# Recommendation tower on one core: a second GpSimd chunk in each third layer, the top MLP on pairs of tiles

## What is computed

```python
x0 = xk = e                       # (2048, 32, 16), gathered rows
outs = []
for W in (W0, W1, W2):            # (32, 32, 64), (32, 64, 64), (32, 64, 64)
    xk = relu(einsum('bmd,bhd,mhk->bkd', x0, xk, W))
    outs.append(sum(xk, axis=2))  # over the 16 dims
h = concatenate([outs..., dense_ctx], axis=1)      # 192 + 16
h = maximum(h @ W_top1 + b_top1, 0.0)              # 512
h = maximum(h @ W_top2 + b_top2, 0.0)              # 256
y = h @ W_top3                                     # 1
```

## Time and profile before

| what | us |
|---|---|
| median of 3 runs (lowest, highest) | 1177.24 (1174.41, 1178.77) |
| the profiled execution, whole | 1176.1 |
| the profiled execution, span of its instructions | 1174.3 |

### The profile page before, as it was taken

One profiled execution on the slowest core, in us unless ns is written; L12 is line 12 of the kernel. 1 busy time (PEld: TensorE's weight loads), 2 busy tenths in 40 slices (PEclk: granted clock), 3 DMA queues, 4 the chain that ended last, 5 costly groups with the idle time before them and its releaser, 6 DMA issues.

```text
span 1174.3 us, 15688 instructions
## 1 busy us (share of the span) xinstructions
PE 1123.1 (96%) x5370; PEld 399.2 (34%) x5370; DVE 1114.6 (95%) x511; ACT 822.5 (70%) x2259; POOL 913.6 (78%) x639
## 2 busy tenths in 40 slices
PE   0779999999999999999999999999999999999998
PEld 0222223333333333333333333333333333333343
DVE  1679999999999999999999999999999999999995
ACT  0346656867868686786877868587776859678674
POOL 6788788888888888888888888888888888885400
PEclk9999999999999999999999999999999999999999
DMA  6788657876666786667787766678766668866300
GB/s 146 206 205 171 133 116 165 174 156 135 132 143 145 166 175 143 137 126 149 149 174 154 150 138 138 135 163 174 153 143 133 141 143 166 174 144 138 66 1 1
DMA packets 78335, 167.31 MB, mean 142 GB/s; under 512 B 22096, under 2 KB 39904, under 8 KB 78256
## 3 DMA queue, kind: packets, MB, share of 16 engines
q1 hardware_dynamic: 59248, 157.76, 61.3%
q0 software_dynamic: 16384, 4.23, 3.8%
q10 hardware_dynamic: 2624, 4.34, 1.3%
HBM read 157.86 MB, written 8.40 MB: 142 GB/s over the span
## 4 chain that ended last, share of the span: by engine, by line
PE 87%; POOL 5%; DVE 3%; issue 3%; ACT 2%; DMA 0%; SPq 0%; DVEq 0%; POOLq 0%
PE acc L762 81%; POOL x_rows L347 4%; DVE p_dve L657 3%; PE acc L866 3%; ACT xb L415 2%; PE acc L852 1%; PE acc L854 1%; PE acc L874 1%; DVE z L684 0%; POOL p_pool L374 0%; ACT x_s L423 0%; ACT xa L406 0%; DMA first_s<-in_first_row 0%; ACT out_l L519 0%; ACT h L550 0%
## 5 line engine op out<-in xcount | busy, mean ns | idle before, releaser
L762 PE MATMUL acc<-p_dve,w_s 128*64 128x512 f32 x3840 | 855.6, 595 | 19.8 <-DVE p_dve L657 19.7
L347 POOL DMA_INDIRECT x_rows<-in_table,ids_s x512 | 492.7, 962 | 146.2 <-issue 131.8
L657 DVE TENSOR_TENSOR p_dve<-spread,xb 128x3072 f32<-128x3072 f32 (+2 forms) x225 | 566.0, 2572 | 3.9 <-issue 3.9
L657 DVE TENSOR_TENSOR p_dve<-spread,xa 128x2048 f32<-128x2048 f32 (+1 forms) x192 | 495.5, 2634 | 9.5 <-ACT xa L406 4.3
L762 PEld LDWEIGHTS acc<-p_dve,w_s 128*64 128x64 f32 x3840 | 271.2, 137 | 554.7 <-issue 485.7
L415 ACT ACTIVATE xb<-acc 32x512 f32<-32x512 f32 x512 | 288.8, 564 | 49.0 <-DVE p_dve L657 42.6
L363 POOL TENSOR_TENSOR p_l<-spread,q_tile 128x2048 f32<-128x2048 f32 x59 | 268.5, 4580 | 8.4 <-DMA q_tile<-x_of_steps 7.4
L406 ACT ACTIVATE xa<-acc 64x512 f32<-64x512 f32 x256 | 145.9, 570 | 158.2 <-PE acc L762 116.9
L374 POOL TENSOR_TENSOR p_pool<-spread,x_s 128x1024 f32<-128x1024 f32 x64 | 152.3, 2379 | 89.3 <-PE acc L762 47.1
L423 ACT ACTIVATE x_s<-acc 64x512 f32<-64x512 f32 x256 | 151.3, 591 | 11.7 <-ACT y_row L569 4.7
L762 PE MATMUL acc<-p_l,w_s 32*64 32x512 f32 (+1 forms) x600 | 139.7, 601 | 0.0
(11 more groups left out here) (26 smaller groups left out, 233.3 us busy)
## 6 DMA issues: line engine op xcount, KB each, us to landing
spread<-x_of_steps SPq DMA_DIRECT2D x244, 512.0 KB, 16.9
q_tile<-x_of_steps SPq DMA_DIRECT2D x120, 128.0 KB
x_rows<-in_table,ids_s POOLq DMA_INDIRECT x512, 4.4
x_of_steps<-x_rows SPq DMA_DIRECT2D x60, 128.0 KB, 1.8
spread<-x_of_steps ACTq DMA_DIRECT2D x4, 512.0 KB, 10.7
spread<-x_of_steps SPq DMA_DIRECT2D x6, 256.0 KB, 5.2
w_s<-in_w SPq DMA_DIRECT2D x2, 512.0 KB, 5.8
spread<-x_of_steps SPq DMA_DIRECT2D x8, 128.0 KB, 3.2
```

Source lines behind the costliest of these rows:

```text
L347: nc.gpsimd.indirect_dma_start(out=x_rows[:, s % 2, i * DIM:(i + 1) * DIM], out_offset=None, in_=table, in_offset=bass.IndirectOffsetOnAxi ...
L657: nc.vector.tensor_tensor(p_dve[:, to:to + n, :], spread[:, s % 3, tile:tile + n, :], over(x[:], n), ALU.mult).then_inc(dve_made, n)
L762: last = nc.tensor.matmul(halves(acc[b * K:(b + 1) * K, :]), w, of_block(prod, b), start=start, stop=stop)
```

## The change

Five edits in one:

1. POOL makes chunks 6 and 7 of layer 3, not 7 alone, from step 1 on; `p_pool` becomes a ring of two. DVE makes 14 chunks there. PE takes both POOL chunks behind chunk 11.
2. `p_dve` has nine slots, not ten. As 15 + 14 products a turn don't fit it, DVE's instruction is cut in two where it would cross the ring's end.
3. ACT takes the first layer's sums of all steps from 4 on; their second half is moved behind `out_1`.
4. The squares are computed on all 128 partitions, with zero weights for the 96 that aren't needed.
5. The MLP works on pairs of tiles (256 columns): tile 0 alone, seven pairs, tile 15 alone. A pair's work is four parts, one to a turn, behind chunk 5 of layer 2: two halves of the first MLP layer (8 matmuls each), the second (16), the third (2). The matmuls of a pair have 64 columns of weights and 256 of data.

```diff
-POOL_CHUNK = NT - 1
-CD = CL - 1
-RING = 10
+RING, POOL_RING = 9, 2
...
-GROUPS_L2 = [(0, 2), (2, 3), (5, 2), (8, 3), (11, 1), (12, 2), (14, 2)]
+GROUPS_L2 = [(0, 2), (2, 3), (5, 1), (8, 3), (11, 1), (12, 2), (14, 2)]
+GROUPS_L2_OF_0 = [(0, 2), (2, 3), (5, 2), (8, 3), (11, 1), (12, 2), (14, 2)]
...
-MLP1_AFTER, MLP2_AFTER, MLP3_AFTER = 5, 5, 13
+LAST_GROUP = TILES // 2
+MLP_AFTER = 5
...
-LATE_MLP1_AFTER, LATE_MLP2_AFTER, LATE_MLP3_AFTER = 4, 15, 6
+LAST_PAIR_AFTER = {1: 0, 9: 1}, {4: 2, 12: 3}
+def mlp_part_of_turn(s):
+    group, part = divmod(s - 4, 4)
+    return (group, part) if s >= 4 and (group, part) != (0, 3) else None
...
 def sums_by_act(s):
-    return s % 2 == 1 and s >= 5
+    return s >= 4
...
+def pool_chunks(s, layer):
+    return (NT - 2, NT - 1) if layer == 2 and s > 0 else (NT - 1,)
...
-        p_pool = sb("p_pool", [P, COLS])
+        p_pool = sb("p_pool", [P, POOL_RING, COLS])
...
             def product(s, layer):
-                n = pool_from(s, layer)
                 pool.wait_ge(x1s_ready if layer == 1 else x2s_ready, s + 1)
                 if layer == 1:
                     pool.wait_ge(b_loaded[s % 3], 16 * Q * (s // 3 + 1))
-                if n > 0:
-                    pool.wait_ge(pool_used, n)
-                nc.gpsimd.tensor_tensor(p_pool[:], spread[:, s % 3, POOL_CHUNK, :], x_s[:, layer - 1, :],
-                                        ALU.mult).then_inc(pool_made, 1)
+                for n, c in enumerate(pool_chunks(s, layer), pool_from(s, layer)):
+                    if n >= POOL_RING:
+                        pool.wait_ge(pool_used, n + 1 - POOL_RING)
+                    nc.gpsimd.tensor_tensor(p_pool[:, n % POOL_RING, :], spread[:, s % 3, c, :],
+                                            x_s[:, layer - 1, :], ALU.mult).then_inc(pool_made, 1)
...
-                nc.scalar.activation(p_l0[0:FIELDS, CP, :], q_tile[0:FIELDS, :],
-                                     ACT.Square).then_inc(squares_made, 2)
+                nc.scalar.activation(p_l0[:, CP, :], q_tile[:], ACT.Square).then_inc(squares_made, 2)
...
-                if sums_by_act(s):
-                    sums_0(s, 1)
...
                 if s >= 1:
                     x2_s(s - 1)
                     out_1(s - 1)
+                if sums_by_act(s) and s + 1 < STEPS:
+                    sums_0(s, 1)
...
             def products(s, layer, c, n):
-                i = dve_from(s, layer) + dve_slot(c)
-                if i + n > RING:
-                    dve.wait_ge(dve_used, i + n - RING)
+                i = dve_from(s, layer) + dve_slot(s, layer, c)
                 to, tile = i % RING, c % NT
+                if to + n > RING:
+                    products(s, layer, c, RING - to)
+                    products(s, layer, c + RING - to, n - (RING - to))
+                    return
+                if i + n > RING:
+                    dve.wait_ge(dve_used, i + n - RING)
...
                 if c == (POOL_AFTER_L2 if s > 0 else POOL_AFTER_L2_OF_0):
-                    pe.wait_ge(pool_made, pool_from(s, 2) + 1)
-                    contract(acc2, w2_s[:, POOL_CHUNK, :], p_pool[:], False, False
-                             ).then_inc(pool_used, 1)
+                    for n, chunk in enumerate(pool_chunks(s, 2), pool_from(s, 2)):
+                        pe.wait_ge(pool_made, n + 1)
+                        contract(acc2, w2_s[:, chunk, :], p_pool[:, n % POOL_RING, :], False, False
+                                 ).then_inc(pool_used, 1)
...
+            def blocks(out, terms):
+                for i, (w, x) in enumerate(terms):
+                    for b in range(2):
+                        last = nc.tensor.matmul(out[b * K:(b + 1) * K, :], w[:, b * K:(b + 1) * K], x,
+                                                start=i == 0, stop=i == len(terms) - 1)
+                return last
...
+            def mlp_pair(step, group, part):
+                if part < 2:
+                    z_is_there(group)
+                acc0_is_free(step, mlp_before(group) + part)
+                for n in range(2):
+                    out = acc0[:, n * 2 * P:(n + 1) * 2 * P]
+                    if part < 2:
+                        cols = slice((2 * part + n) * P, (2 * part + n + 1) * P)
+                        last = blocks(out, ((wt1[:, 0, cols], z_all[:, 0, :]),
+                                            (wt1[0:TOP, 1, cols], z_all[0:TOP, 1, :])))
+                    elif part == 2:
+                        last = blocks(out, [(wt2[:, k, n * P:(n + 1) * P], h1[:, k, :])
+                                            for k in range(H1 // P)])
+                if part == 3:
+                    last = last_layer(2 * P)
                 last.then_inc(mlp_made, 1)
```

More of the change, by code:

```diff
@@ new lines, in evict, with store_y @@
+            def evict(group, part, h, chunks, bias, n_cols):
+                act.wait_ge(mlp_made, mlp_before(group) + part + 1)
+                for i, n in enumerate(chunks):
+                    last = nc.scalar.activation(h[:, n, 0:n_cols], acc0[:, i * n_cols:(i + 1) * n_cols], ACT.Relu,
+                                                bias=bias[:, n:n + 1])
+                last.then_inc(mlp_done, 1)
+            def store_y(group, part, n_cols):
+                n = mlp_before(group) + part + 1
+                act.wait_ge(mlp_made, n)
+                nc.scalar.activation(y_row[:, 0:n_cols], acc0[0:1, 0:n_cols], ACT.Copy).then_inc(mlp_done, 1)
+                act.wait_ge(mlp_done, n)
+                tiles = tiles_of(group)
+                act.dma_start(y[:, tiles.start * P:tiles.stop * P], y_row[:, 0:n_cols]).then_inc(y_stored, 16)
@@ L602, in _ @@
                     squares(s + 1)
-                if t >= 0 and even:
-                    mlp1(t)
-                if t >= 0 and not even:
-                    mlp2(t)
-                if sums_by_act(s):
-                    sums_0(s, 1)
+                if mlp_part_of_turn(s):
+                    group, part = mlp_part_of_turn(s)
+                    (mlp_pair if group > 0 else mlp_single)(group, part)
                 if s == STEPS - 1:
@@ L613, in _ @@
                     x2_b(s - 1)
+                if s == STEPS - 1:
+                    mlp_pair(LAST_GROUP - 1, 0)
                 if s == 1:
                     squares(2)
-                if t >= 0 and not even:
-                    mlp3(t)
                 if s >= 1:
@@ L638, in _ @@
             move_z2(TILES - 1)
-            mlp1(TILES - 1)
-            mlp2(TILES - 1)
-            mlp3(TILES - 1)
-            act.wait_ge(y_stored, 16 * TILES)
+            for part in range(3):
+                mlp_single(LAST_GROUP, part)
+            act.wait_ge(y_stored, 16 * (LAST_GROUP + 1))
         @block.vector
@@ L773, in layer0 @@
                 for c in CP, *range(CP):
-                    rows = P if c < CP else FIELDS
                     if c == CP:
@@ new lines, in mlp_single @@
+            def mlp_single(step, group, part):
+                t = tiles_of(group).start
+                if part == 0:
+                    z_is_there(group)
+                acc0_is_free(step, mlp_before(group) + part)
+                if part == 0:
+                    for n in range(H1 // P):
+                        cols = slice(n * P, (n + 1) * P)
+                        nc.tensor.matmul(acc0[:, cols], wt1[:, 0, cols], z_all[:, 0, z_cols(t)],
+                                         start=True, stop=False)
+                        last = nc.tensor.matmul(acc0[:, cols], wt1[0:TOP, 1, cols], z_all[0:TOP, 1, z_cols(t)],
+                                                start=False, stop=True)
+                elif part == 1:
+                    for n in range(H2 // P):
+                        cols = slice(n * P, (n + 1) * P)
+                        for k in range(H1 // P):
+                            last = nc.tensor.matmul(acc0[:, cols], wt2[:, k, cols], h1[:, k, 0:P],
+                                                    start=(k == 0), stop=(k == H1 // P - 1))
+                else:
+                    last = last_layer(P)
@@ L884, in _ @@
             for s in range(STEPS):
-                t = s // 2 - 2
-                even = s % 2 == 0
                 for c in range(CL):
                     layer1(s, c)
-                    if t >= 0 and even and c == MLP1_AFTER:
-                        mlp1(t)
-                    if t >= 0 and not even and c == MLP2_AFTER:
-                        mlp2(t)
-                    if t >= 0 and not even and c == MLP3_AFTER:
-                        mlp3(t)
+                    if c == MLP_AFTER and mlp_part_of_turn(s):
+                        group, part = mlp_part_of_turn(s)
+                        (mlp_pair if group > 0 else mlp_single)(s, group, part)
                     if s == 0 and c in L0_OF_1_AFTER:
```

247 lines of the change are left out of this document (129 added, 118 removed).

## The result

The changed kernel takes 1211.15 us (median of 4 runs, 1210.39 to 1214.69) against 1176.7 us for the kernel before in the same comparison: a ratio of 1.0297, 95% interval 1.0273 to 1.0322. By that ratio it is 3.0% slower. The profiled execution has a span of 1209.9 us; the prediction's sum for that span was 1207.6.

The account below looks back on a forecast made before the run. PE set the pace, DVE level, POOL one microsecond a turn to spare. With POOL's turn at 35.88 us, 1134.9 + 71.7 + 1.0 gave a span of 1207.6, with 1.8 around it 1209.4; predicted 1210 us, range 1200 to 1220.

Parts of the forecast that it names:

- the prediction's sum: Whole kernel: third chunk of the last first layer at 1134.9, plus 71.7 to the end, plus 1.0, a span of 1207.6.
- step on POOL: Steady part: one product more lengthens POOL's turn from 33.53 to 35.88 us, above PE's 33.75, so POOL sets the pace.
- 11 us of "idle" in two turns: POOL, steady part: busy shares show 11 us to spare, but waits leave one a turn; pauses between gathers fill the rest.
- loop over DRAM: POOL's inputs: no loop is longer than POOL's own turn; `q_tile` lands 33.2 us into a turn, needed at 35.9.
- 1.8 and 3.7 forecast: PE: times in us claimed for the 256-column MLP parts, the big one being 32 records at 0.115.
- 33.7 a turn, as forecast: PE, steady part: it needs 33.75 us a turn (33.6 to 34.1), 0.8 less than the period before.
- the forecast 2.1 us: PE, first layer and behind chunk 11 of layer 3: waits for POOL of about 2.1 us a turn together.
- the third rival: PE's clock falls after idling: one fall a turn stays hidden, two make PE's turn 37.1 and 1245 us; chance 3%.
- the second: POOL and DVE shut each other out: each new POOL product stops DVE for 2.35 us, at worst 1232 us; chance 2%.
- +1.0 less the squares' 0.3: Tail: MLP records cost 8.4 us against 7.5, +1.0; wider squares take away up to 0.3 of PE's time.

Follow-up runs that it names:

- one_pool_chunk: The changed kernel with edit 1 undone, so POOL makes one chunk of layer 3 again: 1173.74 us, ratio 0.9972 to the kernel before.
- pool_alone_c: The kernel before with edits 1 and 2 alone (second POOL chunk, rings of nine and two): 1209.50 us, ratio 1.0268.
- ring9_alone: The kernel before with only the rings changed, nine slots for DVE and two for POOL: 1213.69 us, ratio 1.0029 on a late-starting chip.
- gather15: The changed kernel with 15 gathers a step in place of 16 from step 2 on: 1178.03 us, ratio 1.0009 to the kernel before.

## Why the prediction was right

Its step on POOL decided it and held to 0.04 us: a turn of 35.92 for 35.88, turn 3 at 155.7 for 155.5, turn 29 at 1089.5 for 1088.4. one_pool_chunk and pool_alone_c show the cause from both sides: without the second chunk 37 us are gone; with it and the rings alone the kernel takes 1209.50, within 2 us of the changed one, and the rings alone cost at most a fraction of that (ring9_alone, 1.0029).

The sum was 2.3 us short of the span. Turn 29 came 1.1 late, and 1.0 of that was left when PE reached the third chunk of the last first layer, at 1135.9 (1133.27 + 3 x 0.86) for 1134.9; the other 1.3 are in the tail. That 1210 lies within 1.2 us of 1211.15 is in part luck: 0.6 was added to the sum's 1209.4 because the profiled execution of before lay below its median, and that of the changed kernel, 1211.75, lies 0.6 above its own.

The reading behind it, that 11 us of "idle" in two turns hide only 2, held: gather15 shows the pauses to be part of a gather's cost. The chain of waits of the changed kernel gives 29% of the span to DMA (`q_tile` above all) and might have spoken for a loop over DRAM; one_pool_chunk changes no DMA and is 37 us faster, so that loop doesn't set the pace.

PE: parts of 16 and 32 records took 1.74 and 3.45 us for the 1.8 and 3.7 forecast, the last part 0.96 for 0.56 (`L955`, 1153.11 to 1154.07), which makes 33.7 a turn, as forecast. PE's idle is less than the forecast 2.1 us: it is busy for 68.32 of 71.80 us (600.00 to 671.80), so idle for 1.7 a turn. The starts give more: from 628.88 to 642.45 PE takes 13.57 us for 52 records, 11.16 us of work at 0.2146 each, so 2.4 are lost in this turn; the profile shows 1.75 of them as idle. Its clock stayed at 1.00 in the steady part (mean of the run 0.997), so the third rival didn't come about. Nor did the second: POOL's products last 2354 to 2402 ns in all 95 cases, and DVE's of 3072 columns 3355 at most, as before.

The Trainium skill (SBUF - State Buffer, "Who interferes with whom") has two-input DVE instructions contend with GpSimd ones that read SBUF. The changed kernel has 31 more such products beside DVE's, none stretched; the trace disagrees with the page, as before.

The tail cost 2.1 us more than before (76.6 from the last first layer to the end, against 74.5), for +1.0 less the squares' 0.3: the last MLP part, twice 0.96 for 0.56, and a wait of 0.70 for ACT (`out_l`, at 1180.77) are most of the rest.

A later theory of mine fell in part. That a turn takes the longer of PE's and DVE's needs is right with nine slots (34.7 expected, 34.74 found) and wrong with ten (34.45 expected, 34.32 found; 34.15 at least, and 34.10). One slot is 0.86 us of PE's work, and the needs alternate by 0.7 to 1.7 us.

## What to carry to other kernels

An engine's slack is the waits that end in front of its instructions, summed over a turn, not one minus its busy share: here 1.0 us against an apparent 5.5. Before work is moved to an engine, add it to that engine's turn and compare with the turn of today; work above the slack is paid in full, every turn, and hides every gain made elsewhere in the same change. When two engines are level on average but not turn by turn, try the depth of the ring between them: here nine slots paid most of the maximum of each turn, and ten nearly the mean.

## What the runs showed that was not expected

One slot of the ring is worth some 0.21 us a turn: 34.74 for 34.53 alone, 34.31 for 34.10 with edits 3 to 5, each pair across two chips. Beside the kernel before on its own chip the second pair is clear of noise, 0.9972 (0.9963, 0.9982) for 0.9914 (0.9900, 0.9927); the first isn't. Of its 0.21, 0.14 are DVE's own need (34.15 for 34.01), where the odd ring cuts instructions in two. Making the 32-partition chunk 128 partitions wide, with zero weights, gives 0.30 us in the turns that PE sets (34.57 for 34.87), and 0.5% of the time (0.9934 to 0.9961), though it multiplies by more rows. Why the narrow chunk costs more, no run shows.
